# Cross-attention scores on all 128 rows of TensorE: keys as stacks of high and low parts of one head, queries doubled, put there by transfers within SBUF

## What is computed

```python
q = (queries @ wq_w + wq_b).reshape(B, S, H, DK).transpose(0, 2, 1, 3)
k_proj = keys @ wk_w + wk_b
v_proj = values @ wv_w + wv_b
k_ext = jnp.concatenate([k_proj, jnp.broadcast_to(mk, (B, MEM, H * DK))], axis=1)
v_ext = jnp.concatenate([v_proj, jnp.broadcast_to(mv, (B, MEM, H * DV))], axis=1)
k = k_ext.reshape(B, T, H, DK).transpose(0, 2, 1, 3)
v = v_ext.reshape(B, T, H, DV).transpose(0, 2, 1, 3)
scores = jnp.einsum('bhsd,bhtd->bhst', q, k) / jnp.sqrt(jnp.float32(DK))
attn = jax.nn.softmax(scores, axis=-1)
out = jnp.einsum('bhst,bhtd->bhsd', attn, v)
```

## Time and profile before

| | us |
|---|---|
| median of 3 runs | 1515.9 (1514.07 to 1521.61) |
| the profiled execution, its own time | 1514.06 |
| its span, first to last instruction | 1512.2 |
| of it cross attention with all engines filled | 161 to 643 |

### The profile page before, as it was taken

One profiled execution on the slowest core, in us unless ns is written; L12 is line 12 of the kernel. 1 busy time (PEld: TensorE's weight loads), 2 busy tenths in 40 slices (PEclk: granted clock), 3 DMA queues, 4 the chain that ended last, 5 costly groups with the idle time before them and its releaser, 6 DMA issues.

```text
span 1512.2 us, 27707 instructions
## 1 busy us (share of the span) xinstructions
PE 1355.4 (90%) x9290; PEld 1093.8 (72%) x9290; DVE 1110.2 (73%) x2430; ACT 930.7 (62%) x2302; POOL 830.5 (55%) x866
## 2 busy tenths in 40 slices
PE   4888999999999999956999999878899998999991
PEld 4666777777777777645899999734556565899991
DVE  4898766666666766646688886389898996779935
ACT  4776565555655556534488884147788883548853
POOL 3675454444444444431688875138796885048850
PEclk9999999999999999975899999979999999999996
DMA  4100000000000000034566657674444340227784
GB/s 153 43 29 8 29 9 8 2 8 2 8 9 1 9 1 1 2 120 183 191 230 228 226 210 233 231 267 136 143 155 145 129 140 14 96 85 250 260 270 177
DMA packets 52942, 167.85 MB, mean 111 GB/s; under 512 B 13178, under 2 KB 22340, under 8 KB 44996
## 3 DMA queue, kind: packets, MB, share of 16 engines
q1 hardware_dynamic: 45316, 145.63, 27.3%
q0 software_dynamic: 7488, 20.46, 4.2%
HBM read 149.28 MB, written 16.78 MB: 110 GB/s over the span
## 4 chain that ended last, share of the span: by engine, by line
PE 34%; POOL 8%; DVE 7%; issue 4%; ACT 2%; DMA 1%; POOLq 0%; DVEq 0%; SPq 0%; ACTq 0%
PE m_ps L1756 10%; PE m_ps L1779 10%; POOL s_hc L2082 5%; PE m_ps L1753 2%; PE m_ps L1774 2%; PE s_yps L2517 2%; DVE s_h L2452 1%; PE m_ps L1736 1%; PE s_yps L2629 1%; DVE tokens L1624 1%; DMA table<-m_xn 1%; PE m_ps L1704 1%; ACT s_dps L2161 1%; PE m_ps L1660 1%; PE m_ps L1715 0%
## 5 line engine op out<-in xcount | busy, mean ns | idle before, releaser
L306 POOL TENSOR_TENSOR a_pexp<-a_pexp,a_rsum 128x384 f32<-128x384 f32 (+1 forms) x320 | 245.9, 787 | 289.7 <-DVE a_rsum L523 289.6
L396 ACT ACTIVATE a_pexp<-a_ps,a_nmax 128x384 f32<-128x384 f32 (+1 forms) x320 | 180.9, 566 | 175.8 <-DVE a_nmax L519 175.0
L519 DVE TENSOR_REDUCE a_nmax<-a_ps 128x1 f32<-128x384 f32 (+1 forms) x320 | 153.6, 521 | 61.5 <-PE a_ps L620 60.4
L2082 POOL TENSOR_TENSOR s_hc<-s_h,s_bc_rows 128x1024 f32<-128x1024 f32 x64 | 151.0, 2361 | 53.6 <-DVE s_h L2452 53.1
L1756 PE MATMUL m_ps<-m_xT,m_w1s 128*128 128x256 f32 x1032 | 155.1, 287 | 2.1 <-DVE m_xT L1509 2.1
L1779 PE MATMUL m_ps<-m_w2s,m_hs 128*128 128x256 f32 x1032 | 152.1, 283 | 0.0
L1103 POOL DMA_INDIRECT m_xrow<-table,m_row_from x78 | 83.6, 1072 | 118.9 <-DVE m_row_from L1451 85.7
L2452 DVE TENSOR_TENSOR_SCAN s_h<-s_dps,s_inp 128x512 f32<-128x512 f32 x128 | 148.8, 1203 | 0.0
L636 PE MATMUL a_ps<-a_ident,a_pexp 128*128 128x128 f32 x896 | 143.9, 273 | 3.6 <-ACT a_pT L255 3.0
L1756 PEld LDWEIGHTS m_ps<-m_xT,m_w1s 128*128 128x128 f32 x1032 | 137.0, 193 | 2.8 <-DVE m_xT L1509 2.5
L1779 PEld LDWEIGHTS m_ps<-m_w2s,m_hs 128*128 128x128 f32 x1032 | 135.6, 191 | 0.0
(11 more groups left out here) (442 smaller groups left out, 3562.9 us busy)
## 6 DMA issues: line engine op xcount, KB each, us to landing
s_bc_rows<-s_bc_table SPq DMA_DIRECT2D x64, 512.0 KB, 3.7
arrived<-in_down SPq DMA_DIRECT2D x29, 1024.0 KB, 8.1
arrived<-in_up SPq DMA_DIRECT2D x23, 1024.0 KB, 5.8
m_w<-in_up SPq DMA_DIRECT2D x16, 512.0 KB, 5.7
m_w<-in_down SPq DMA_DIRECT2D x16, 512.0 KB, 5.0
carried_up<-in_up SPq DMA_DIRECT2D x8, 512.0 KB, 5.9
carried_down<-in_down SPq DMA_DIRECT2D x8, 512.0 KB, 6.7
arrived<-results SPq DMA_DIRECT2D x3, 1024.0 KB, 8.5
```

What stands on the lines that cost most here:

```text
L306: nc.gpsimd.tensor_tensor(pexp[:, r, 0:n], pexp[:, r, 0:n], rsum[:, r:r + 1].to_broadcast([128, n]), ALU.mult).then_inc(normed, 1)
L396: nc.scalar.activation(pexp[:, r, 0:n], ps_s[score_bank(u)][:, 0:n], ACT.Exp, bias=nmax[:, r:r + 1], accum_out=sums[:, r:r + 1]).then_inc( ...
L519: nc.vector.tensor_reduce(nmax[:, u % RING:u % RING + 1], ps_s[score_bank(u)][:, 0:keys_of(u)], AX.X, ALU.max, negate=True).then_inc(maxed, 1)
L2082: nc.gpsimd.tensor_tensor(halves(hc[:, u % HC_RING, :]), halves(h[:, u % H_RING, :]), bc_rows[:, u % BC_RING, 1, :].unsqueeze(1).to_broadc ...
```

## The change

For each head the keys become one stack of 128 rows: the 64 rows of the high part and under them the 64 rows of the low part (`k_stack`, 384 keys wide). The queries are doubled: a stack holds the same 64 rows twice, once for the high part and once for the low part (`q_stack`, a ring of three pairs). One matmul on 128 rows then gives a part of the queries times (high + low) of the keys. `scores` issues four matmuls of 128 rows, two for head 0 and then two for head 1, instead of six of 64 rows. The product low times low is computed too. Self attention keeps its six.

ACT and DVE no longer write keys and queries where PE reads them, but to one of four slots (`move_slots`), high and low part side by side. SP then moves them with four transfers within SBUF for each job (`move`): 64 partitions each, 1 KB a partition for keys (64 KB), 2 KB for queries (128 KB). There are 128 jobs, so 512 transfers. ACT waits before it writes a slot until the job four before has landed, and PE waits in `scores` for the landing (`wait_moved`) instead of `k_low` and `q_low`. The memory keys get into the stacks by four transfers, once, behind which SP issues the load of `wq`. The load of `wox` keeps its condition and goes to another place; the loads of context are now issued between the moves, in the order of the jobs. The slots lie in memory that self attention uses earlier.

```diff
+                half, as_bytes = lambda h: slice(64 * h, 64 * h + 64), lambda a: a.bitcast(fp32)
                 for n, free_after in (("mk", "wo0"), ("wv", "wk"), ("wq", "wv")):
+                    if n == "wq":
+                        sp.wait_ge(w_low, SPLIT_DONE["mk"])
+                        for h in range(2):
+                            for part in range(2):
+                                sp.dma_start(as_bytes(k_stack[half(part), :, h, S:KEYS]), as_bytes(k_stack[half(h), :, part, 0:MEM])).then_inc(mk_moved, 16)
                     sp.wait_ge(w_low, SPLIT_DONE[free_after])
                     sp.dma_start(staged[n], w[n]).then_inc(w_loaded[n], 16)
...
+                sp.wait_ge(mk_moved, 64)
+
+                def move(kind, b):
+                    n, p = MOVE[kind, b], int(kind[1])
+                    src, done = move_slots[n % MOVE_SLOTS], moved[n % MOVE_SLOTS]
+                    sp.wait_ge(k_low if kind[0] == "k" else q_low, PX * b + p + 1)
+                    for h in range(2):
+                        for part in range(2):
+                            if kind[0] == "k":
+                                sp.dma_start(as_bytes(k_stack[half(part), p, h, 0:S]), src[half(h), part, :]).then_inc(done, 16)
+                            else:
+                                sp.dma_start(as_bytes(q_stack[(PX * b + p) % Q_SLOTS][half(part), h, :, :]), src[half(h), :, :]).then_inc(done, 16)
...
-                        nc.scalar.activation(ks[0][:, p, 0:S], bank[:, 0:S], ACT.Identity, bias=bkx[:, p:p + 1]).then_inc(high, 1)
...
+                        n, p, bias = MOVE[kind, b], int(kind[1]), bkx if kind[0] == "k" else bqx
+                        if n >= MOVE_SLOTS:
+                            wait_moved(act, n - MOVE_SLOTS)
+                        nc.scalar.activation(move_slots[n % MOVE_SLOTS][:, 0, :].bitcast(fp32r), bank[:, 0:S], ACT.Identity, bias=bias[:, p:p + 1]).then_inc(high, 1)
...
-                        pe.wait_ge(k_low, (u - NS) // 4 + 1)
-                        pe.wait_ge(q_low, (u - NS) // 4 + 1)
-                        q, k = [t[:, p % Q_RING, :] for t in qs], [t[:, p, :] for t in ks]
+                        wait_moved(pe, MOVE[f"k{p}", (u - NS) // UX])
+                        wait_moved(pe, MOVE[f"q{p}", (u - NS) // UX])
                     if u >= 2:
                         pe.wait_ge(exped, u - 1)
+                    if u >= NS:
+                        for h in range(2):
+                            for part in range(2):
+                                last = nc.tensor.matmul(ps_s[score_bank(u + h)][:, 0:n], q_stack[(u - NS) // 4 % Q_SLOTS][:, h, part, tok(s)], k_stack[:, p, h, :],
+                                                        start=(part == 0), stop=(part == 1))
+                            last.then_inc(scores_raw, 1)
+                        return
```

More of the change, by code:

```diff
@@ L50, in sem, with place_of @@
             return sems[-1]
+        def place_of(n, shape, dt=fp32):
+            with nc.sbuf_tensor(f"a_{n}", shape, dt) as t:
+                return t
         def pair_of(n, shape):
@@ L75, in attention_layers @@
         cT = pair_of("cT", [128, KD, S])
-        qs = pair_of("qs", [128, Q_RING, S])
+        q_stack = [sb(f"q_stack{n}", [128, 2, 2, S], fp32r) for n in range(Q_SLOTS - 1)]
         oTs = pair_of("oTs", [128, P0, S])
+        moved_b = place_of("moved_b", [128, 2, 2, S])
         scratch = sb("scratch", [128, ND * 2 * D + V_BUFS * ND * D])
@@ L181, in attention_layers @@
                         HIGH[kind, b] = len(HIGH)
+        MOVES = [(kind, b) for v in range(FIRST, END) for kind, b in DONE_AT.get(v, []) if kind[0] == "k" or kind in [f"q{p}" for p in range(PX)]]
+        MOVE = {job: n for n, job in enumerate(MOVES)}
         LAST_IN_PT_BANK = max(b for kind, b in BANK if kind == "pv" and BANK[kind, b] == LAST_PT_BANK)
@@ L190, in attention_layers @@
                   "wk": vx[:, 0:KD, :], "wv": vx[:, 0:KD, :], "wq": vx[:, 0:KD, :],
-                  "wox": scratch[:, 0:PX * D].rearrange("p (k n) -> p k n", k=PX)}
+                  "wox": scratch[:, ND * 2 * D:ND * 2 * D + PX * D].rearrange("p (k n) -> p k n", k=PX)}
         split = {"wo0": wo0, "wk": [t[:] for t in wk], "wv": [t[:] for t in wv], "wq": [t[:] for t in wq],
-                 "mk": [t[:, :, S:KEYS] for t in ks], "wox": wox}
+                 "mk": [k_stack[:, :, part, 0:MEM] for part in range(2)], "wox": wox}
         def chunk_of(name, c, a):
@@ new lines, in _ @@
+                for v in range(FIRST, END):
+                    for kind, b in DONE_AT.get(v, []):
+                        if (kind, b) == ("q4", 0):
+                            sp.wait_ge(o_raw, SELF_PAIRS)
+                            sp.dma_start(staged["wox"], w["wox"]).then_inc(w_loaded["wox"], 16)
+                        if (kind, b) in MOVE:
+                            move(kind, b)
+                        elif kind == "ctxT" and b + 1 < B:
+                            sp.wait_ge(job_raw, NUMBER[kind, b] + 1)
+                            sp.dma_start(cx[:], token_rows(ctx_in, b + 1)).then_inc(ctx_loaded, 16)
```

26 lines of the change are left out of this document (12 added, 14 removed).

## The result

| us | before | changed |
|---|---|---|
| median | 1516.98 (1514.07 to 1521.61, 4 runs) | 1501.56 (1500.72 to 1506.07, 4 runs) |
| profiled execution, its span | 1514.06, 1512.2 | 1506.07, 1504.3 |
| scores of cross attention, first to last | 161.4 to 642.8 | 163.2 to 632.1 |

The ratio is 0.9907, 95% interval 0.9884 to 0.993: faster by 15.4 us, where 1500 had been forecast. In six further runs, beside 17 of the kernel before on one chip, the ratio was 0.9914 (0.989 to 0.9938), a gain of 12.2 us.

What follows compares the result with a forecast made beforehand. PE's instructions one behind another were taken to bound cross attention. 16 us saved on scores, less 1 at the end, moves covered: 1514.1 - 15 = 1499 us, stated as 1500, range 1491 to 1515 for 8 in 10.

Steps and rivals of the forecast that it cites:

- The bound: In cross attention PE is busy 470 of 482 us, so 1 us less on PE is 1 us less in the end.
- The scores: Cross attention: four 128-row matmuls of 384 columns take 0.70 us, saving 0.22 behind transposes and 0.03 behind the 64-column matmuls.
- rival 3: Border costs of a scores pass come from semaphore waits, not shape; the fourth round adds 22 us, 1536 us; chance 0.05.
- The sum: Whole kernel: 16 us gained on scores less 1 at the end, 1514.1 - 15 = 1499 us, stated as 1500.
- The range: Time of the whole kernel, meant for 8 in 10: 1491 to 1515 us.
- rival 1: Moves clog SP's burst and ACT waits for slots; at 1 us a transfer 1554 us; chance 0.08.
- rival 4: More gained: cheaper border behind the 64-column matmuls or shorter stands for exponentials; half of both gives 1492 us; chance 0.09.
- rival 2: q5's move alone lands late, 8 us instead of 4; PE stands 18 us in all, 1518 us; chance 0.09.
- The moves on SP: 512 transfers at 0.47 us an issue, 1.9 us a move against one job each 2.1; 1 us late at most.
- The slot wait: ACT's wait for the job four before; the burst's ninth job has 3.8 us of cover, so no cost.
- The bound for a move: From 3.05 us of SP per move, 0.76 a transfer, ACT's lateness eats the gain of 1.9 us a sequence.
- q5: Shortest way to PE's scores: lands in 3.1 to 4.1 us, cover 6.0, last sequence 3.8; wait 0 to 0.3 us once.

## Why the prediction was right, and where not

- The bound: right. 1.85 us less in PE's passages of a steady sequence was 1.83 us less in its length.
- The scores: 4 x 0.175 = 0.70 us was taken, between bounds of 0.64 and 0.76. Measured 0.175, and the passages 0.94 and 1.23 us against 0.93 and 1.24 forecast. Reading 384 columns off the line through 256 and 512 was exact here. One sign of rival 3 appeared without it: the first step of the scores behind transposes is 0.26 us, over the 0.25 that had been named. It was a poor sign, since the step ahead of it is 0.03; the last step, 0.175, and the run with a fourth round rule rival 3 out.
- The sum: 15 us forecast, 15.4 in the medians, and that close an agreement is partly luck. The second comparison gave 12.2 us, the kernel without moves 12.9, and in the one trace of each kernel the scores of cross attention are 12.6 us shorter. The passages as they were measured make 64 x (0.211 + 0.020) = 14.8 us, where the sum had 16. The first, second and last sequence gave 0.9, 1.5 and 1.1 us, not 1.85, 2.1 us less together, where the sum took off 1. The trace began 1.8 us later too; already at 31 us, far ahead of the change, it was 2.1 us behind, and the second trace of the changed kernel was not, so that is scatter of the start.
- The range: 1491 to 1515 us was said to leave out rivals 1 and 3 and half of rival 4, but it leaves out rival 2's own 1518 too. By the chances given it held about 0.74, not 8 in 10.
- The Trainium skill, TensorEngine Tiling (Array Packing), recommends row tiling under Performance Considerations when the contraction is 64 or less; by that, as an estimate with the measured round, three rounds against four, the change would have cost 22 us. In this kernel the runs show the opposite. What outweighs the round the same page has under Key Properties, a drain when the tiling mode changes, and there the traces agree: 0.39 and 0.20 us a pass with equal rounds, against 0.175 for a round.
- The moves on SP: the step that was mis-sized. 0.47 us an issue was taken from loads at the start; it is 0.64, so 2.57 us a move and not 1.9. The other row at hand, five loads 0.75 us apart, had been put down to their bytes, and half the bytes changed nothing; but that row was no better a source, for its single steps are 0.48, 0.65, 1.23, 0.74 and 0.67 us. "SP just keeps up, 1 us late at most" was wrong; SP is 5.6 us late, 1.2 of it by the slow issue. From low part to landing, 6.5 us in the median instead of 3.1 to 4.1.
- The slot wait cost PE nothing, as forecast, but ACT did wait, which had been named as a sign of rival 1. The bound for a move, 3.05 us, lay above the 2.57 measured. In the sequence shown k1's move landed 15.8 us after q5's low part (375.36 to 391.17), and ACT, which would have written 15.6 us after it, stood 0.29 us. Without the slow issue of 1.8 us the landing would have come at 14.6, so the margin that the bound promises is what such an issue uses up. Rival 1 had a chance of 0.08; the run with six transfers for keys shows that 1.28 us more in five of nine moves cost 7 us a sequence, and by rival 1's formula (three moves of 2.57, two of 3.85, 2 to land, cover 15.3) ACT would be only 2.1 us late. What the prediction left out is q0's way to its reader: 10.5 us from low part to landing, and 0.46 us left. A chance of 0.2 would have been nearer to what the rows allowed.
- q5: ahead of it SP is idle, as predicted; its landing came 4.1 us after its low part (375.37 to 379.49), its cover was 6.0; over the eight sequences it is 4.1 to 5.6 us. In the last sequence PE stood 0.44 us longer than usual ahead of the scores of pair 5; 0 to 0.3 had been forecast.
- The Trainium skill, SBUF — State Buffer, section on the DMA port swizzle, gives 64 partitions at most about 218 GB/s. 128 KB in 0.64 us are 205 GB/s, just under; but 64 KB have the same 0.64 us, and 128 partitions too, so this limit is not what is seen.

## What to carry to other kernels

Count changes of tile shape on TensorE like instructions: with short jobs around it, a pass in the shape of its neighbours can be faster with a third more rounds. Before hiding transfers behind work, compare their issue time in a burst, taken from a crowded stretch of the queue, with the interval at which they are asked for, and give the margin of each waiter as a number; here it was nothing for ACT and 0.5 us for PE. And on a saturated engine a wait removed is worth its length only if the next resource (another bank, the next transfer) is looked at too: twice here it took all or part back.

## What the runs showed of the hardware

- A change between 64-row and 128-row matmuls costs about 0.2 us at each border at the upper clock level: 0.39 us per excursion from 128 rows and back. A visit to the 64-column shape costs 0.35 us.
- SP issues a load of context in 0.38 us when it stands alone, and one transfer each 0.64 us in a burst, whatever the size (32 to 128 KB), the partitions (64 or 128) and the side the data come from (SBUF or HBM). One issue in 22 takes 1.0 to 2.0 us instead of 0.6.
- An engine that waited for a landing goes on 0.08 to 0.10 us after it.
- A transfer within SBUF lands 2.0 us after its issue for 64 KB and 2.3 to 2.4 for 128 KB, next to 2.3 for 64 KB from HBM in the same place of the burst.
